# Opening loads of a batched graph network: two issuing queues, and another order of the opening's splits

## What is computed

```python
h  = adj @ (x @ W0 + b0) / adj.sum(-1)        # neighbours, averaged
x1 = layernorm(x + h)
y  = relu(adj @ (x1 @ W1) + b1)
y  = relu(adj @ (y  @ W2) + b2)
y  = adj @ (y @ W3) + b3
out = layernorm(x1 + y)
```

## Time and profile before

| | us |
|---|---|
| median of 3 runs | 549.39 (549.17 to 550.0) |
| the profiled execution | 549.95 |
| its span, first to last instruction | 548.1 |
| TensorE, matmuls busy | 535.5 |
| VectorE busy | 347.2 |
| ScalarE busy | 307.0 |
| GpSimd busy | 212.2 |

### The profile page before, as it was taken

The page is one execution under the profiler, slowest core; times in us unless marked ns, Lnnn a source line. Parts: engine busy times, 40 slices in busy tenths (PEclk is TensorE's granted clock), DMA queues, the critical chain, the costliest instruction groups (busy, mean ns, idle before and its releaser), DMA issues.

```text
span 548.1 us, 10688 instructions
## 1 busy us (share of the span) xinstructions
PE 535.5 (98%) x3695; PEld 494.6 (90%) x3695; DVE 347.2 (63%) x1029; ACT 307.0 (56%) x757; POOL 212.2 (39%) x228
## 2 busy tenths in 40 slices
PE   7889999999999999999999999999999999999996
PEld 6778999989899898999989899898998989899896
DVE  4864665756657475665756657475674756657546
ACT  4556646566554756655566554756655566554532
POOL 2865409062260814509063270814509063271100
PEclk9999999999999999999999999999999999999999
DMA  7640070612507043070611507033070521500002
GB/s 267 210 158 1 14 257 1 222 48 61 209 0 268 0 126 142 1 266 0 199 68 56 212 0 267 1 117 151 0 268 0 185 84 55 215 2 39 1 1 78
DMA packets 15286, 58.23 MB, mean 106 GB/s; under 512 B 1952, under 2 KB 2720, under 8 KB 13472
## 3 DMA queue, kind: packets, MB, share of 16 engines
q1 hardware_dynamic: 15264, 57.94, 29.3%
HBM read 49.55 MB, written 8.39 MB: 106 GB/s over the span
## 4 chain that ended last, share of the span: by engine, by line
PE 91%; DVE 4%; DMA 2%; ACT 1%; issue 1%; SPq 1%; DVEq 0%
PE bank_a L174 15%; PE bank_a L176 15%; PE bank_a L175 15%; PE bank_b L174 15%; PE bank_b L175 15%; PE bank_b L176 15%; DMA y<-in_xT 2%; DVE x L720 0%; DVE v L713 0%; DVE xT_lo L662 0%; DVE stats L763 0%; ACT std L581 0%; DVE x_lo L662 0%; DVE stats L724 0%; ACT x_hi L560 0%
## 5 line engine op out<-in xcount | busy, mean ns | idle before, releaser
L876 POOL TENSOR_TENSOR adj_lo<-adj_raw,adj_hi 128x512 fp32r<-128x512 f32 x56 | 70.8, 1296 | 267.6 <-ACT adj_hi L482 267.6
L662 DVE TENSOR_TENSOR x_lo<-bank_a,x_hi 128x512 fp32r<-128x512 f32 x62 | 42.9, 692 | 67.6 <-ACT bank_a L562 67.6
L174 PE MATMUL bank_b<-h_hi,adj_hi 128*128 128x256 f32 (+1 forms) x256 | 71.0, 277 | 1.6 <-DVE h_lo L662 1.5
L537 ACT ACTIVATE std<-moments,eps_col 128x1 f32<-128x1 f32 x64 | 18.9, 295 | 94.4 <-DVE moments L733 94.4
L175 PE MATMUL bank_b<-h_lo,adj_hi 128*128 128x256 f32 (+1 forms) x256 | 70.8, 277 | 0.0
L176 PE MATMUL bank_b<-h_hi,adj_lo 128*128 128x256 f32 (+1 forms) x256 | 70.8, 277 | 0.0
L176 PE MATMUL bank_b<-s_hi,adj_lo 128*128 128x256 f32 x232 | 64.1, 276 | 0.0
L174 PE MATMUL bank_b<-s_hi,adj_hi 128*128 128x256 f32 x232 | 64.0, 276 | 0.0
L175 PE MATMUL bank_b<-s_lo,adj_hi 128*128 128x256 f32 x232 | 64.0, 276 | 0.0
L560 ACT ACTIVATE x_hi<-bank_a,b_col 128x512 fp32r<-128x512 f32 x62 | 42.4, 684 | 21.6 <-PE bank_a L176 20.4
L858 POOL TENSOR_TENSOR x1b<-x,b_all 128x256 f32<-128x256 f32 x64 | 46.1, 753 | 17.5 <-DVE x L720 17.5
(11 more groups left out here) (135 smaller groups left out, 1667.8 us busy)
## 6 DMA issues: line engine op xcount, KB each, us to landing
adj_raw<-in_adjT SPq DMA_DIRECT2D x30, 512.0 KB, 5.4
adj_rows<-in_adj SPq DMA_DIRECT2D x14, 1024.0 KB, 9.3
x_raw<-in_x SPq DMA_DIRECT2D x15, 512.0 KB, 7.4
out_y<-y SPq DMA_DIRECT2D x15, 512.0 KB, 2.9
xT_raw<-in_xT SPq DMA_DIRECT2D x14, 512.0 KB, 6.5
w_raw<-in_w SPq DMA_DIRECT2D x4, 256.0 KB, 10.0
adj_rows<-in_adjT SPq DMA_DIRECT2D x2, 512.0 KB, 9.7
xT_raw<-in_xT SPq DMA_DIRECT2D x2, 256.0 KB, 4.8
```

Of the source, the lines that this page charges most:

```text
L174: pe.matmul(acc, st[0], mv[0], start=start, stop=False)
L537: act.activation(std1[:, j:j + 1], moments1[:, j, 1:2], ACT.Sqrt, bias=eps_col[:, :]).then_inc(std1_ready, 1)
L662: return dve.tensor_tensor(lo, full, hi.bitcast(F32), ALU.subtract)
L876: pool.tensor_tensor(adj_lo[:, s, k, :], raw[:, k, :], adj_hi[:, s, k, :].bitcast(F32), ALU.subtract).then_inc(adj_split, 1)
```

## The change

SyncE and ScalarE both issue loads now. SyncE's queue: xT of graph 0 in one transfer, the low half of adj, x, b0, the low half of adj1, W1, b3, W2, b1, b2, W3. ScalarE's queue: w0 and the high half of adj first, then, behind the wait for `eps_set` and the first Sqrt, xT1, the high half of adj1, x1. xT of graph 0 has one semaphore, and xT1 gets one of its own.

ScalarE's order changes: both halves of xT and h of tiles 0 and 1 come before the first adj_hi, and h of tiles 2 and 3 each one place earlier against the adj_hi; x1_hi(0) comes ahead of std_1(FIRST, 1), adj_hi(3) and h of graph 1; x1_hi(1) comes between h(second) of tiles 1 and 2; h(second, 3) comes behind std_1(FIRST, 2); g of graph 0 comes ahead of std_1(second, 0). VectorE takes h_lo of tile 2 before adj_lo(1) of graph 0. GpSimd takes x1_lo(0) behind two adj_lo of graph 1 instead of three, and x1_lo(1) behind three instead of four. The arithmetic and TensorE's program are the same.

```diff
--- before.py
+++ after.py
@@ -89,7 +89,7 @@
 
         w_loaded = [sem(f"w{n}_loaded") for n in range(4)]
         b_loaded = [sem(f"b{n}_loaded") for n in range(4)]
-        xT0_loaded = [sem(f"xT0_half{n}_loaded") for n in range(2)]
+        xT1_loaded = sem("xT1_loaded")
         xT_loaded = sem("xT_loaded")
         x_loaded = sem("x_loaded")
         adj_loaded = [sem(f"adj_half{n}_loaded") for n in range(2)]
@@ -205,22 +205,13 @@
                 return slice(half * n // 2, (half + 1) * n // 2)
 
             sp.sem_inc(rows_ready, 2 * T)
-            sp.dma_start(w_raw[:, 0, :, :], w0).then_inc(w_loaded[0], DMA)
-            for half in range(2):
-                tiles = half_of(half, T)
-                sp.dma_start(xT_raw[:, tiles, :], xT[0, :, tiles, :]).then_inc(xT0_loaded[half], DMA)
-
-            for half in range(2):
-                tiles = half_of(half, T)
-                sp.dma_start(adj_raw[:, tiles, :], adjT[0, :, tiles, :]).then_inc(adj_loaded[half], DMA)
+            sp.dma_start(xT_raw[:, :, :], xT[0]).then_inc(xT_loaded, DMA)
+            low = half_of(0, T)
+            sp.dma_start(adj_raw[:, low, :], adjT[0, :, low, :]).then_inc(adj_loaded[0], DMA)
             sp.dma_start(x_raw[:, :, :], x[0]).then_inc(x_loaded, DMA)
             sp.dma_start(b0_all[:, :], b0.partition_broadcast(P)).then_inc(b_loaded[0], DMA)
-            sp.dma_start(xT1_raw[:, :, :], xT[1]).then_inc(xT_loaded, DMA)
-            for half in range(2):
-                tiles = half_of(half, T)
-                sp.dma_start(adj1_raw[:, tiles, :], adjT[1, :, tiles, :]).then_inc(adj1_loaded[half], DMA)
+            sp.dma_start(adj1_raw[:, low, :], adjT[1, :, low, :]).then_inc(adj1_loaded[0], DMA)
             sp.dma_start(w_raw[:, 1, :, :], w1).then_inc(w_loaded[1], DMA)
-            sp.dma_start(x1_raw[:, :, :], x[1]).then_inc(x1_loaded, DMA)
             sp.dma_start(b3_all[:, :], b3.partition_broadcast(P)).then_inc(b_loaded[3], DMA)
             sp.dma_start(w_raw[:, 2, :, :], w2).then_inc(w_loaded[2], DMA)
             sp.dma_start(b1_col[:, :], b1).then_inc(b_loaded[1], DMA)
@@ -489,10 +480,13 @@
             def split_xT(nxt, half):
 
                 tiles = slice(half * T // 2, (half + 1) * T // 2)
-                if nxt is FIRST:
-                    act.wait_ge(xT0_loaded[half], DMA)
+                if nxt is second:
+                    act.wait_ge(xT1_loaded, DMA)
+                elif nxt is FIRST:
+                    act.wait_ge(xT_loaded, DMA)
                 else:
                     act.wait_ge(xT_loaded, at(nxt, DMA, 0))
+                if nxt is not FIRST:
                     act.wait_ge(p0_done, at(nxt, T, 0))
                 raw = xT1_raw if nxt is second else xT_raw
                 copy_hi(xT_hi[:, tiles, :], raw[:, tiles, :]).then_inc(xT_hi_ready, 1)
@@ -601,16 +595,22 @@
                     s2(new)
                     norm1(nxt, before(new, -2) if ahead else None)
 
+            high = slice(T // 2, T)
+            act.dma_start(w_raw[:, 0, :, :], w0).then_inc(w_loaded[0], DMA)
+            act.dma_start(adj_raw[:, high, :], adjT[0, :, high, :]).then_inc(adj_loaded[1], DMA)
             act.wait_ge(eps_set, 1)
             act.activation(sqrt_eps[:, :], eps_col[:, :], ACT.Sqrt)
+            act.dma_start(xT1_raw[:, :, :], xT[1]).then_inc(xT1_loaded, DMA)
+            act.dma_start(adj1_raw[:, high, :], adjT[1, :, high, :]).then_inc(adj1_loaded[1], DMA)
+            act.dma_start(x1_raw[:, :, :], x[1]).then_inc(x1_loaded, DMA)
             split_xT(FIRST, 0)
             split_xT(FIRST, 1)
+            h(FIRST, tiles=range(0, 2))
             split_adj(FIRST, 0)
-            h(FIRST, tiles=range(0, 1))
+            h(FIRST, tiles=range(2, 3))
             split_adj(FIRST, 1)
-            h(FIRST, tiles=range(1, 3))
+            h(FIRST, tiles=range(3, T))
             split_adj(FIRST, 2)
-            h(FIRST, tiles=range(3, T))
             split_adj(FIRST, 3)
             split_xT(second, 0)
             split_xT(second, 1)
@@ -618,20 +618,21 @@
             std_1(FIRST, 0)
             split_adj(second, 1)
             split_adj(second, 2)
+            x1_split_hi(FIRST, 0)
             std_1(FIRST, 1)
             split_adj(second, 3)
-            h(second, bank_a, range(0, 1))
-            x1_split_hi(FIRST, 0)
-            h(second, bank_a, range(1, T))
+            h(second, bank_a, range(0, 2))
+            x1_split_hi(FIRST, 1)
+            h(second, bank_a, range(2, 3))
             std_1(FIRST, 2)
-            x1_split_hi(FIRST, 1)
+            h(second, bank_a, range(3, T))
             split_w(1)
             std_1(FIRST, 3)
             x1_split_hi(FIRST, 2)
             x1_split_hi(FIRST, 3)
-            norm1(second, None, range(0, 1))
             g(FIRST, 0)
             g(FIRST, 1)
+            norm1(second, None, range(0, 1))
             split_w(2)
             split_w(3)
             act.wait_ge(b_loaded[1], DMA)
@@ -802,9 +803,9 @@
             sub_hi(w_lo[:, 0, :, :], w_raw[:, 0, :, :], w_hi[:, 0, :, :]).then_inc(w0_split, 1)
             split_xT(FIRST, 0)
             split_xT(FIRST, 1)
-            h(FIRST, tiles=range(0, 2))
+            h(FIRST, tiles=range(0, 3))
             split_adj0(1)
-            h(FIRST, tiles=range(2, T))
+            h(FIRST, tiles=range(3, T))
             split_adj0(3)
             split_xT(second, 0)
             split_xT(second, 1)
@@ -900,10 +901,11 @@
             add_b0(FIRST)
 
             pool.wait_ge(adj_split, T)
-            split_adj(second, range(0, 3))
+            split_adj(second, range(0, 2))
             split_x1_first(0)
+            split_adj(second, range(2, 3))
+            split_x1_first(1)
             split_adj(second, range(3, T))
-            split_x1_first(1)
             add_b0(second, range(0, 1))
             split_x1_first(2)
             split_w(1)
```

## The result

The changed kernel takes 546.78 us (median of 5, 546.56 to 547.76), the one before 549.39 in the same session (5 runs): a ratio of 0.9953, interval 0.9941 to 0.9965. That is 2.6 us, 0.47%, quicker, just under the range (546.9 to 550.0) and next to rival A (547.1). The profiled execution is the slowest of the five: 547.76 us, span 546.0.

A forecast was written before the change was run, and what follows sets the result against it. TensorE's matmuls were taken as the bound (535.5 of 548.1 us), p4's start as yardstick. Gains 0.45 (VectorE's chain) + 0.5 (g's order) = 0.95: profiled 549.95 to 549.0, median 548.4; own range 547.8 to 549.0, wide range 546.9 to 550.0.

The forecast's parts named there:

- rival A: Opening loads: transfers get quicker, b0, adj and x all land 1.3 us earlier; 547.1 us, chance 0.27.
- step 4: GpSimd: add_b0 starts at 15.35, x1_lo(0) begins at 21.2, so p2_first(0) starts at 22.05, 0.93 us earlier.
- step 2: TensorE's p1_first starts at 12.8 instead of 11.92; p0(second) ends 0.75 us later, hidden by 1.92 us idle behind it.
- step 6: p2_first(2) and (3) wait for VectorE's chain through x1(2); starts 27.5 and 29.05, gain 0.45 us.
- step 3: VectorE: xT_lo pair of graph 1 takes 1.85 instead of 2.34 us; norm1 and h_lo come 0.45 us earlier.
- Equal turns: Opening loads: the two queues are served alike; both halves of adj land together at 10.7, b0 at 15.3.
- rival B: Opening loads: unequal turns favour ScalarE's queue, adj's low half lands late; at 13.0 the time is 550.7 us; chance 0.12.
- 1.: ScalarE: issuing five DMAs takes 2.3 to 3.3 us, covered because nothing is due before xT lands; cost 0.
- 5.: p1(second, 0) waits 0.8 us for the fourth adj_lo, ready at 25.2; most handed back, gain 0.25 us.
- 7.: ScalarE: g ahead of std_1(second, 0) removes TensorE's 0.56 us gap before p3; gain 0.5 us.
- 8.: TensorE: p3 to p4 keeps its 5.1 us, a wait for relu and x2_lo; SyncE's loop loads cost 0.
- Rival C's clock: TensorE: longer idling before p1_first lowers the clock, costing 2 us, over half covered; 549.2 us; chance 0.18, shared with VectorE-GpSimd hindrance.

The follow-up runs named there:

- the repeat: The changed kernel, unaltered, timed and profiled once more beside other variants on one chip: 546.84 us, ratio 0.9954.
- one queue again: Second profile of the changed kernel with all loads on SyncE's queue in the old order, xT still whole: 548.21 us, one execution.
- filler kernel: The changed kernel with 16 unused matmuls on zeros between p0_first and p1_first on TensorE: 547.90 us, ratio 0.9968.

## Why the prediction was wrong, and where it was right

**The step that failed is the landing times,** taken from the bytes ahead at the rate of before; the one on which p4 hangs is b0's, in "b0 stands fourth on SyncE's queue beside adj1's high half: 3.375 MiB, 15.3". It came at 14.2: add_b0 started at 14.19 instead of 15.35. From there step 4's arithmetic holds, and the error passes through nearly unchanged. The fourth adj_lo was ready at 23.95 instead of 25.2, p2_first(2) started at 26.35 instead of 27.5, and p4 at 36.19 instead of 37.3, 1.1 us sooner.

adj's landing was wrong in the same way: "Both halves of adj land together at 1.75 MiB", 10.7, against a start of adj_hi(0) at 9.29, and p1_first at 12.8 against 11.41. The range's early end for it (9.4) was passed too. But that term does not enter the sum, since step 2 had its lateness hidden, and rightly: with adj's halves changed over p1_first starts at 10.66, and p4 moves only with GpSimd's chain. The path in step 6 was wrong in part as well. p2_first(2) hung on GpSimd's fourth adj_lo, through x1(2), and not on the 0.45 us of step 3.

What both landings had at nothing was the joining of xT's halves and the second queue: 341 GB/s from 3.5 to 6.5 us instead of 173. With xT in halves adj_hi(0) starts at 10.57, p1_first at 12.70 and p4 at 37.20, each within 0.13 of the forecast for the changed kernel. The match is in part luck: b0 was there at 14.46, 0.9 sooner than forecast, and the four add_b0 took 3.97 instead of 3.35. It was rival A's mechanism, "One 4 KB row of xT instead of two of 2 KB, with two queues to draw from", at about rival A's price: b0 and adj's low half shifted by 1.2 and 1.4 us, and A had 1.3 for every step behind them. My argument against A, that adj is read at the same place, had no row behind it, and the range cut A off at 1.5 us under the forecast. That accounts for 1.1 us of a miss of 1.6. Another 0.1 is in the profiled executions (549.0 forecast, 547.76 measured, where p4 gives 1.1). The last 0.4 is in the step from a profile to the median: I took 0.56 between them and it was 0.98. No profile of a quick execution of the changed kernel was taken, so what makes those quick stays open.

**Equal turns.** adj's high half landed at 7.1, the low one at 9.2, the order that rival B feared; B's loss did not come since everything behind xT was earlier. That order does not speak against equal turns. My sums had paired the transfers of the two queues one by one. Counted by bytes, equal turns bring w0 in at 0.5 MiB, xT at 1.0, adj's high half at 1.5, its low half at 2.0 and b0 at 3.25, which is the order measured. By the landings of before, 2.0 MiB would be there near 11.5 us (an estimate: 10.8, and 0.25 of the 1.125 MiB that took the next 3.3 us). It was 9.2, so it is the rate that was missed. The Trainium skill's rule in "DMA: Bandwidth & Descriptors", section Issuing engines are not separate DMA queues (only issuing time is saved) is not borne out in this stretch: with xT whole, 341 and 403 GB/s from two queues against 250 and 268 from one, at a DMA share of 0.95 and more in all four windows. What that is worth at the end is less sure, 1.6 us by medians from different chips and nothing clear by the profiles.

Step by step:
1. ScalarE's five issues cost 0: right. Each took 0.39 to 0.99 us, and they were done by 3.65, before xT landed at 4.96.
2. "That is hidden by the 1.92 us idle behind it": right. p0(second) ended at 21.46 (21.8 forecast), and the cover was used by the halved clock rather than by a late adj.
3. xT_lo 1.85 instead of 2.34: it took 1.28. It started at 13.44 instead of 14.8, and both halves were made before b0 let GpSimd begin.
4. add_b0 15.35 and x1_lo(0) 21.2 forecast; 14.19 and 19.95 measured. The four took 3.25 (3.35 forecast). The arithmetic is right; its input, b0's landing, is the term that failed.
5. The wait for adj_lo in p1(second, 0), 0.8 us: 0.18 in the changed kernel's profile, where TensorE's clock held it back. In three profiles at clock 1.00 it is there: 0.60 with the halves changed over, 0.61 with one queue, 0.62 with xT in halves. Right.
6. The chain of norm1 is earlier, by more than the 0.45 forecast (it starts at 15.70; before it was 17.06), but it is not what p2_first(2) hung on.
7. g ahead of std: the gap of 0.56 goes, and comes back at 0.56 when g is put back; at p4 it is 0.49. Right. The time rose by more (0.9974 against 0.9953, 1.1 us), on another chip and without an explanation.
8. p3 to p4 keeps its 5.1 us: 5.15. Right.

**The parts don't add up.** Loads alone are worth 1.4 us (0.0025), orders alone 0.4 (between 1.2 quicker and 0.4 slower); together 2.6. With the loads alone p4 is 1.43 us earlier, since x1_lo(0) ends at 21.48 instead of 22.93. With the orders alone GpSimd loses 0.68 us twice to x1 and x1_hi, which its own adj_lo had held up, and that eats their gain in the profiled execution. Whether the quicker half of its executions had no such meetings is not shown.

**Rival C's clock** did come: 15 matmuls from 12.23 to 15.45 at 0.215 us instead of 0.12 lose 1.4 us of TensorE's work. At the end it cost nothing that the profiles show: by the last table p4 stands 12.23 or 12.24 us behind the fourth adj_lo in the three with a fall of the clock and g in its new place, and 12.22 to 12.26 in the six without. The waits for GpSimd had covered it. Of the 11 executions of the changed kernel in both sessions, the eight with a mean clock of 0.999 or 1.000 took 546.56 to 546.86 and once 547.98; the three at 0.996 or 0.997 took 547.76, 547.59 and 546.64. That looks like an effect but is a weak test. Nine of 11 fit, and with xT in halves executions at 0.995 and at 1.000 took the same 548.8 to 549.1.

## What to carry to other kernels

Judge a change to opening loads by when the operand lands on which the chain to the yardstick hangs. Here that was b0, which GpSimd needs, and not adj, for which TensorE waits first. Try the size of the transfers (one whole load against two halves) apart from the number of queues: here each raised the opening rate and both had been priced at nothing, and xT's halves alone made 1.9 us in the medians and 1.0 at p4. An order written out by hand is tuned to landing times, so time new loads and new orders both alone and together. Before an item is moved ahead of another on an engine, see who makes its input and what that producer can be held up by. With the old loads, GpSimd's moved x1_lo waited for an x1 that GpSimd itself had held up.

## What the runs showed of the hardware that I had not expected

- Two transfers of 256 KB with rows of 2 KB took until 7.9 us where one of 512 KB with rows of 4 KB took until 5.0 to 5.5, in the same queue with the same neighbours. Why the engines falter on the first (264 against 341 to 403 GB/s) stays open; no run separated the length of the rows from the number of transfers.
- A load of b0 right behind xT costs its neighbours: with b0 there, the rate from 6.5 to 8 us was 281 GB/s at a DMA share of 0.77, against 412 at 1.01 in the kernel that differs only in b0's place (halves changed over). Windows of the two, b0 early first:

```profile
6.50:8.00 1.50, 1.50 (x14) 1.42 (x13) 1.05 (x3) 0.56 (x2) 0.00 (x0) 1.00 0.77 281
```

```profile
6.50:8.00 1.50, 1.50 (x12) 1.37 (x13) 1.09 (x3) 0.66 (x2) 0.00 (x0) 1.00 1.01 412
```

- TensorE's granted clock fell to 0.50 some 0.7 us after it had resumed from an idle time of 2.49 us (changed kernel), and likewise, 0.3 to 1.5 us after resuming, behind 1.96, 1.92, 1.81 and 2.03 us in four other profiles (the repeat, x1 moves taken back, g behind std, one queue again). It stayed at 1.00 behind 1.78 us (loads alone), 1.46 (before) and 1.08 (halves changed over). With xT in halves the idle time was 2.09 us and the clock stayed at 1.00 up to 22 us, so idle time alone does not decide it.
- The granted clock of a window can read 1.00 where the trace has no record of it. In the filler kernel 19 matmuls took 3.98 us from 5.9 to 9.9, half the pace of later ones, under a clock of 1.00 (the window is shown with that kernel). The first record of the clock in that trace is at 10.0 us, just where the pace doubles, while in the others it is at 4.3 to 7.0. So a clock of 1.00 in a window ahead of the first record says nothing.
- Where VectorE's x1 instruction (0.40 to 0.415 us alone) took longer, from 0.45 to 1.52 us, it ended 0.15 or 0.16 us behind the end of a GpSimd instruction, in 39 of 39 cases in the 14 profiles.
